# First context of a gated block: byte codes written in one operation into preset f16 words

## The reference, cut to what matters

```python
q1 = clip(round(layernorm(x) / s1 + z1), 0, 255)            # 2 x 1024 x 2048
q2 = clip(round(ctx / s2 + z2), 0, 255)                     # 2 x 2048 x 2048
x  = x + tanh(g_xattn) * ((q1 - z1) * s1) @ ((q2 - z2) * s2)
x  = x + tanh(g_ffn) * layernorm(x) @ ((U * S) @ V.T).T     # U, V: 2048 x 512
```

## Time and profile before

| | |
|---|---|
| median of 3 runs | 601.6 us (601.25 to 601.85) |
| span of the profiled execution | 600.8 us |
| TensorE busy | 583.0 us (97%) |
| VectorE, ScalarE, GpSimd busy | 384.5, 210.5, 193.5 us |
| first matmul | 11.34 us |

### The profile page before, as it was taken

How to read it: one execution, slowest core, us unless ns; L and a number is a source line. 1 busy time by engine, 2 the same in 40 slices (tenths; PEclk the granted TensorE clock), 3 DMA queues, 4 the chain that set the end, 5 groups by cost and what they waited for, 6 DMA issues and landing times.

```text
span 600.8 us, 7536 instructions
## 1 busy us (share of the span) xinstructions
PE 583.0 (97%) x2800; PEld 266.3 (44%) x2800; DVE 384.5 (64%) x703; ACT 210.5 (35%) x256; POOL 193.5 (32%) x149
## 2 busy tenths in 40 slices
PE   1999999999999999999999999999999999999998
PEld 0444444444444444445444444444444444444444
DVE  6968999995288962855266975647375665735212
ACT  4799877822041432476422220303011030301000
POOL 2998850002223419735505800210404030030000
PEclk9999999999999999999999999999999999999999
DMA  8999995539828896979934432360917355171512
GB/s 275 387 387 386 308 262 127 109 122 196 242 54 230 192 217 189 274 264 327 235 123 140 102 73 54 75 189 12 211 42 157 106 97 166 32 161 35 123 53 105
DMA packets 145940, 102.74 MB, mean 171 GB/s; under 512 B 108784, under 2 KB 109040, under 8 KB 145904
## 3 DMA queue, kind: packets, MB, share of 16 engines
q1 hardware_dynamic: 136912, 84.96, 53.6%
q10 hardware_dynamic: 8992, 17.30, 8.8%
HBM read 58.99 MB, written 16.78 MB: 126 GB/s over the span
## 4 chain that ended last, share of the span: by engine, by line
PE 74%; DVE 12%; DMA 7%; issue 3%; ACT 1%; SPq 1%; POOL 1%; ACTq 0%; DVEq 0%
PE bank L556 27%; PE bank L587 14%; PE bank L654 8%; PE bank L653 8%; PE bank L658 8%; PE bank L592 7%; DMA v_hl<-in_ctx_dram 4%; DVE u_hl L1249 2%; DVE ring L1134 2%; DVE xn L1171 1%; DVE xs L1174 1%; DVE v_hl L1243 1%; DMA qT<-qn 1%; PE bank L519 1%; DMA ring<-in_x_dram 1%
## 5 line engine op out<-in xcount | busy, mean ns | idle before, releaser
L556 PE MATMUL bank<-q,qT 128*128 128x512 bf16 x896 | 202.1, 381 | 0.6 <-DVE ring L1134 0.3
L556 PEld LDWEIGHTS bank<-q,qT 128*128 128x128 bf16 x896 | 87.7, 98 | 107.9 <-issue 1.8
L260 POOL TENSOR_SCALAR ring<-ring,bvec 128x2048 f32<-128x2048 f32 x16 | 33.3, 2084 | 270.2 <-DVE bvec L1116 270.2
L587 PE MATMUL bank<-v_hl,xT 128*128 128x512 f16 x512 | 115.8, 379 | 0.0
L265 POOL TENSOR_TENSOR ring<-ring,corr 128x512 f32<-128x512 f32 x64 | 88.7, 1417 | 24.6 <-ACT corr L851 23.6
L1134 DVE SCALAR_TENSOR_TENSOR ring<-bank,const,ring 128x512 f32<-128x512 f32 x64 | 47.6, 743 | 57.9 <-PE bank L556 57.8
L1207 DVE SCALAR_TENSOR_TENSOR ring<-bank,cy,ring 128x512 f32<-128x512 f32 x63 | 46.6, 747 | 56.7 <-PE bank L658 56.6
L654 PE MATMUL bank<-u_hl,hbuf 128*128 128x512 f16 x208 | 78.9, 380 | 0.0
L653 PE MATMUL bank<-u_hl,hbuf 128*128 128x512 f16 x208 | 78.9, 379 | 0.0
L254 POOL TENSOR_SCALAR q<-u8r,const 128x1024 bf16<-128x1024 uint8 x52 | 64.2, 1243 | 39.2 <-ACT u8r L757 35.6
L587 PEld LDWEIGHTS bank<-v_hl,xT 128*128 128x128 f16 x512 | 49.9, 98 | 59.9 <-DMA xT<-xs 0.5
(11 more groups left out here) (136 smaller groups left out, 524.9 us busy)
## 6 DMA issues: line engine op xcount, KB each, us to landing
out_dram<-ring SPq DMA_DIRECT2D x63, 256.0 KB, 3.6
ring<-in_x_dram SPq DMA_DIRECT2D x62, 256.0 KB, 4.1
v_hl<-in_ctx_dram SPq DMA_DIRECT2D x26, 512.0 KB, 11.5
stage<-in_ctx_dram ACTq DMA_DIRECT2D x17, 512.0 KB, 5.5
u_hl<-in_L_ffn_V_dram SPq DMA_DIRECT2D x8, 512.0 KB, 11.4
corr<-in_ctx_dram ACTq DMA_DIRECT2D x8, 512.0 KB, 6.1
stage<-in_ctx_dram SPq DMA_DIRECT2D x6, 512.0 KB, 11.4
q<-in_ctx_dram ACTq DMA_DIRECT2D x4, 512.0 KB, 10.1
```

Of the source, the lines that this page charges most:

```text
L556: mm = nc.tensor.matmul(unit_bank(t, n)[:, :], qT_of(t)[:, k, :], q2[:, n, k, :], start=(k == 0), stop=(k == KT - 1))
L587: nc.tensor.matmul(h_bank(u)[:, :], xT[:, g, half, k % 8, :], v_hl[:, k, 0, :], start=(g == 0 and a == 0 and half == 0), stop=False)
```

## The change

`q2` becomes f16. Ahead of its use every 16-bit word of `q2` is set to 0x6400, which is 1024 in f16. A whole number q from 0 to 255 in the low byte makes the word 1024 + q. So context 0 is converted by one operation, which writes the byte straight into every second byte of `q2` (`q2_low`), and the centre of context 0 and 1 is -1024 as the correction terms see it (`C_C2`).

- GpSimd presets `q2` by four memsets of 128 x 4096 f32 words (`fill(n)`, one for each column block): `fill(0)` and `fill(1)` right behind its small memsets, `fill(2)` and `fill(3)` behind chunk 5.
- One-operation conversions: ScalarE does chunks 6, 7, 8 and the even ones from 10 to 30 (`ON_ACT`, 14 of them), GpSimd chunks 0 to 5 and the odd ones from 9 to 31 (18).
- VectorE converts no chunk any more. It gets one more 128 x 1 operation in `ratios`.
- Context 1 goes as before through `u8r`, with `op2` now adding 1024 and writing f16.
- `qn`, `qT`, the identity and the ones are f16 too; the identity is no longer built a second time (L293 to L297 are gone). The parts of the column sums are scaled by 1/16 instead of 1/4.
- `load_chunk` waits for the one-operation conversion of chunk c - 10.

```diff
+    OFFSET = 1024.0
+    OFFSET_PAIR = 2.0 ** 73 * (1.0 + 200.0 / 2.0 ** 16)
...
-        q2 = sb("q2", [P, NQ, KT, W], bf16)
+        q2 = sb("q2", [P, NQ, KT, W], f16)
...
-        WHOLE = (27, 31)
-        POOL_WHOLE = (1, 2, 3, 4, 5)
+        ON_ACT = (6, 7, 8, 10, 12, 14, 16, 18, 20, 22, 24, 26, 28, 30)
...
+        q2_low = lambda c: q2_chunk(c).bitcast(u8).rearrange("p (w b) -> p w b", b=2)[:, :, 0]
...
+            def fill(n):
+                nc.gpsimd.memset(flat2(q2[:, n, :, :]).bitcast(f32), OFFSET_PAIR).then_inc(q2_filled, 1)
+
+            def op1(c):
+                pool.wait_ge(SPOT[c][1], LANDED[c])
+                pool.wait_ge(q2_filled, c // CQ + 1)
+                if c == 0:
+                    pool.wait_ge(centre_ready, 1)
+                nc.gpsimd.tensor_scalar(q2_low(c), flat2(SPOT[c][0]), C_R2, P_Z2, ALU.mult, ALU.add).then_inc(q2_pool, 1)
...
-            nc.gpsimd.memset(ones_h[:, :], 4.0 / GW).then_inc(setup_ready, 1)
-
+            nc.gpsimd.memset(ones_part[:, :], 16.0 / GW).then_inc(setup_ready, 1)
+
+            fill(0)
+            fill(1)
             for c in range(CQ):
-                if not on_dve(c):
-                    op2(c)
+                if c not in ON_ACT:
+                    op1(c)
+            fill(2)
+            fill(3)
             for n in range(NQ - 1):
-                for i, c in enumerate(range(CQ * (n + 1), CQ * (n + 2), 2)):
-                    op2(c)
+                for i, c in enumerate(range(CQ * (n + 1) + 1, CQ * (n + 2), 2)):
+                    op1(c)
...
@@ scalar
+                if c < CB:
+                    act.wait_ge(q2_filled, c // CQ + 1)
+                    nc.scalar.activation(q2_low(c), flat2(SPOT[c][0]), ACT.Identity,
+                                         bias=P_Z2, scale=C_R2).then_inc(q2_act, 1)
+                    return
...
             root1(0)
-            op1(0)
             act.wait_ge(centre_ready, 1)
             op2(0)
...
@@ vector
                 step(ts(C_C, C_C, MAGIC, None, ALU.subtract))
+                step(ts(C_C2, P_Z2, 0.0, -OFFSET, ALU.mult, ALU.add))
                 ts(C_NC, C_C, -1.0, None, ALU.mult).then_inc(centre_ready, 1)
...
             for n in range(NQ - 1):
-                for i, c in enumerate(range(CQ * (n + 1) + 1, CQ * (n + 2), 2)):
-                    op2(c)
-                    if n == 0 and i == 1:
-                        sums1(3)
-                        variance1(3)
-                    elif n == 0 and i == 3:
-                        quantise(3)
+                if n == 0:
+                    sums1(3)
+                    variance1(3)
+                    quantise(3)
```

More of the change, by code:

```diff
@@ L58, in gated_block_program @@
         corr = sb("corr", [P, D], f32)
-        qn = sb("qn", [P, D], bf16)
-        qT = sb("qT", [P, 2, KT, P], bf16)
+        qn = sb("qn", [P, D], f16)
+        qT = sb("qT", [P, 2, KT, P], f16)
         xn = sb("xn", [P, HW], f32)
@@ L66, in gated_block_program @@
         u8r = sb("u8r", [P, NU8, CK * W], u8)
-        ident_b = sb("ident_b", [P, P], bf16)
+        ident = sb("ident", [P, P], f16)
         ones_f = sb("ones_f", [P, P], f32)
-        ones_b = sb("ones_b", [P, P], bf16)
-        ones_h = sb("ones_h", [P, P], f16)
+        ones = sb("ones", [P, P], f16)
+        ones_part = sb("ones_part", [P, P], f16)
         par = sb("par", [P, 6 + RT], f32)
@@ L188, in gated_block_program @@
         part_count = lambda t, h=1: 2 * t + h + 1 if t < G else 2 * G + t - G + 1
-        WHOLE = (27, 31)
-        POOL_WHOLE = (1, 2, 3, 4, 5)
[L191 to L194, removed]
+        ON_ACT = (6, 7, 8, 10, 12, 14, 16, 18, 20, 22, 24, 26, 28, 30)
+        act_count = lambda c: sum(i <= c for i in ON_ACT)
+        pool_count = lambda c: c + 1 - act_count(c)
+        u8_count = lambda c: c - CB + 1
         unit_bank = lambda t, n: bank[4 * (n % 2) + t] if t < G else bank[(unit(t, n) - NQ * G) % 3]
@@ L291, in _ @@
                         op2(c)
[L292 to L297, removed]
                 if t not in (6, 7):
@@ L316, in load_chunk @@
                 b, n, i = chunk(c)
[L317 to L320, removed]
+                if c >= NST and c - NST in ON_ACT:
+                    sp.wait_ge(q2_act, act_count(c - NST))
                 elif c >= NST:
-                    sp.wait_ge(ctx_u8, act_u8(c - NST))
+                    sp.wait_ge(q2_pool, pool_count(c - NST))
                 sp.dma_start(SPOT[c][0], ctx_k[b, :, CK * i:CK * i + CK, n * W:(n + 1) * W]).then_inc(SPOT[c][1], 16)
@@ L518, in colsum @@
                     if b == 0:
-                        mm = nc.tensor.matmul(colsum_bank(b, n)[:, :], ones_b[:, :], q2[:, n, k, :],
+                        mm = nc.tensor.matmul(colsum_bank(b, n)[:, :], ones[:, :], q2[:, n, k, :],
                                               start=(k == 0), stop=(k == KT - 1))
@@ L522, in colsum @@
                         g = k % CG * GW
-                        mm = nc.tensor.matmul(colsum_bank(b, n)[g:g + GW, :], ones_b[:, g:g + GW], q2[:, n, k, :],
+                        mm = nc.tensor.matmul(colsum_bank(b, n)[g:g + GW, :], ones[:, g:g + GW], q2[:, n, k, :],
                                               start=(k < CG), stop=(k >= KT - CG), tile_position=(0, g))
@@ L531, in colsum_total @@
                 pe.wait_ge(parts_lo, n + 1)
-                nc.tensor.matmul(colsum_bank(1, n)[:, :], ones_h[:, :], part_hi(n), start=True, stop=False)
-                nc.tensor.matmul(colsum_bank(1, n)[:, :], ones_h[:, :], part_lo(n), start=False, stop=True)\
+                nc.tensor.matmul(colsum_bank(1, n)[:, :], ones_part[:, :], part_hi(n), start=True, stop=False)
+                nc.tensor.matmul(colsum_bank(1, n)[:, :], ones_part[:, :], part_lo(n), start=False, stop=True)\
                     .then_inc(colsum_summed, 1)
@@ L789, in qT_half @@
                 nc.scalar.activation(qT_of(t)[:, 8 * h:8 * h + 8, :].rearrange("p k w -> p (k w)"),
-                                     bank[4 + 2 * (t % 2) + h][:, :].bitcast(bf16), ACT.Copy).then_inc(t_read, 1)
+                                     bank[4 + 2 * (t % 2) + h][:, :].bitcast(f16), ACT.Copy).then_inc(t_read, 1)
             def root1(t):
@@ L910, in _ @@
             qT_half(2, 1)
-            for c in range(9, 14):
+            for c in (10, 12, 14):
                 op1(c)
             column_correction(0, 0)
-            op1(14)
             root1(3)
-            for c in range(15, 19):
+            for c in (16, 18):
                 op1(c)
             op2(3)
-            for c in range(19, 23):
+            for c in (20, 22):
                 op1(c)
             column_correction(0, 1)
-            for c in range(23, 27):
+            for c in (24, 26, 28, 30):
                 op1(c)
-            op1(28)
-            op1(29)
-            op1(30)
             column_correction(0, 2)
```

82 lines of the change are left out of this document (26 added, 56 removed).

## The result

The change costs **10.8 us**: 612.57 us (612.05 to 613.23, 4 runs) against 601.73 (601.25 to 602.82, 4 runs) in the same session, a ratio of 1.0178 [1.0164, 1.0192]. The forecast was 606.3, range 600.0 to 608.2. The direction was right, and the time lies 4.4 us above the range.

The account below looks back on a forecast made before the run. But for 0.6 us, the kernel was taken to be paid for in its first 23 us, before TensorE runs gapless. Terms: 5.3 - 0.6 = +4.7 us, span 605.5, plus 0.8 gives 606.3; range 600.0 to 608.2.

Parts of the forecast that it names:

- Fills: GpSimd's memsets of 4096 words: 3.5 us each, bounds 1.7 and 3.9; fill(0) ends at 5.4, fill(1) at 8.9.
- Fills hold VectorE: VectorE's tensor_scalar operations beside a fill: each waits the whole fill; bounds no wait or the whole fill.
- The rival that a memset holds nothing back: Start, L1052 at 5.6: fills do not delay VectorE, so the kernel gets 1.2 us faster, 600.4 us; chance 16%.
- the short fills: Rival on GpSimd's presets: fills take 1.7 us each, done by 5.4, giving 601.0 us; chance 6%.
- Start: VectorE behind fill(0) and fill(1): tile 0's statistics begin at 9.7, not 5.4; tile 1's quantise at 21.4.
- Conversions: GpSimd's one operation a chunk, writing every second byte: 1.19 us, bounds 1.11 and 2.3.
- Every second byte is dear: Rival on the chunk conversions: strided bytes take 2.3 us a chunk on both engines, 3 us on top, 609; chance 7%.
- The step that failed: VectorE's waiting tensor_scalar goes ahead of GpSimd's next operation; tile 1's second half, behind chunk 5, done at 23.9.
- a meeting that falls the other way: Tile 2's quantise waiting when fill(2) ends: one half 3 us sooner, half of that reaching the end; range's low end.
- The path to the end: Tile 2's late halves delay ScalarE's copies; TensorE stands at the ninth matmul until 37.4; chunk 7 at 38.7, +5.3 us.
- The small terms: TensorE's wait for VectorE's chunk goes, -0.6 us; no chunk waits between 40 and 75 us, none for GpSimd's chunks.
- Cost at nothing on GpSimd: Fills on GpSimd alone cost nothing, as it is idle there, waiting for chunk 0.

Follow-up runs that it names:

- best kernel: Changed kernel with single-column `ratios`, chunks 6 and 7 on GpSimd, fill(2) behind chunk 7 and tile 2's quantise, fill(3) behind chunk 17: 600.43 us, ratio 0.9977.
- twelfth run: Changed kernel with one wait added: GpSimd waits on its own semaphore for chunk 5 ahead of fill(2): 606.49 us, ratio to before 1.0076.
- kernel with both cures: Changed kernel with `ratios` in 128x1 operations and fill(2), fill(3) moved behind chunk 9 and tile 2's quantise: 602.07 us, ratio to before 1.0005.
- ninth kernel: The best kernel with fill(3) as VectorE's memset behind its last constants, instead of on GpSimd: 600.59 us, ratio 0.9976.

## Why the prediction was right and where it failed

- **Fills.** 3.5 us each, of a memset's slope: 6.98 and 6.95 for two. Right.
- **Fills hold VectorE.** The decisive term of the sign, taken from no direct row: right for `tensor_scalar` on two or more columns. The rival that a memset holds nothing back falls with L1039's 3.44 us, and the short fills fall too. The Trainium skill ("SBUF — State Buffer", Who interferes with whom) says that the one that issues first has the shared ports for its whole instruction and the other fully blocks; the rows agree inside a memset, which lasts 3.49 us. By the rows' starts they do not agree at the seam behind chunk 5: the half stood from 22.13, fill(2)'s row begins at 23.22, and the fill went first.
- **Start.** Statistics of tile 0 at 9.7 foreseen, at 9.51 measured; quantise of tile 1 at 21.4 and 21.27.
- **Conversions.** 1.19 us for a strided byte: 1.20 measured, 1.20 without the stride. "Every second byte is dear" falls.
- **The step that failed** is the rule that the waiting operation "waits until GpSimd's operation is over, and then goes ahead of GpSimd's next", applied to tile 1's second half: done at 23.9, it said; 30.7 it was. The rule had been read from GpSimd's conversions, and between two of these it holds (1.62 us for the half in the best kernel). Behind a conversion with a fill next it does not hold (8.59 us). That seam alone is worth 6.1 us (the twelfth run), all of what the forecast was short. I had named a meeting that falls the other way, but only for tile 2 and only as a gain, so the range had no room for it above.
- **The path to the end.** The forecast let it run over tile 2's copies, with TensorE standing at the ninth matmul. The chain of waits of after runs over tile 1 (start, duration, what):

```profile
21.27 9.46 DVE qn L1092 x2
...
30.75 1.25 ACT qn L771 x2
...
32.05 1.03 PE bank L489 x8
33.08 2.61 PE bank L549 x6
```

  From 32.05 on TensorE has no gap: all that had queued up behind tile 1's half takes it to chunk 7 at 44.72, 12.7 us, and tile 2, though ScalarE begins its second copy only at 42.20 and not at 36.4, is in time. 1.7 of the 12.7 are the clock: 1.27 on six matmuls and 0.41 on eight transposes (1.03 us, where those of tile 1's first half took 0.62). The forecast had the clock only as a possibility above its sum. So 6.8 us on VectorE became 6.0 at chunk 7.
- **The small terms.** VectorE's chunk wait of 0.6 us is gone, and no chunk is waited for after 40 us: right. That TensorE would wait "no longer for GpSimd's chunks" was wrong by the forecast's own path, which had chunk 0 done at 10.9: the wait ahead of the first matmul is still 11.0. No half of tile 2 lasted 2.5 to 3 us, since the fills were over by then; in the twelfth kernel the first lasts 3.22. The stand at tile 2's ninth matmul did not come, for the reason just given.
- **Span and time.** The span was foreseen at 605.5 and is 610.7, 5.2 more; the time was missed by 6.3. The forecast added 0.8 us for what lies around a span. In every profile with a known time it is 1.8 (612.51 against 610.7, 606.73 against 604.9), so the profiled execution of before took about 602.6 by this estimate, 1.0 above the median, and the spans show the miss too small by that. From median to median 4.7 us were foreseen and 10.8 came: 6.1 more.
- **Cost at nothing on GpSimd.** Nothing in after speaks against it: GpSimd was idle at the start, and in the middle the tiles were later still. Once these are in time, the kernel with both cures is 1.2 us above the one without presets, with waits for GpSimd's `pre` in it.

In the times of the runs: no meetings 600.9; the start's alone 604.5, the middle's alone 605.1; both, with a turn for VectorE between chunk 5 and fill(2), 606.5; without that turn 612.6.

## What to carry to other kernels

A GpSimd operation that reads nothing and lies in its idle time is not free: list VectorE's `tensor_scalar` operations beside it with two or more elements a partition, and who waits for them. Put long fills where VectorE's work has slack, cut VectorE's few-element operations to one column, or put a wait for GpSimd's own last operation ahead of a fill, which cost GpSimd 0.4 us (fills of 7.38 instead of 6.95) and gave 6.1 us here. A rule on who goes first should be read from a row with the same two kinds of operation on both sides of the seam, and where there is none, the range takes the whole train behind it, to the far side too.

## What the hardware showed that I had not expected

- The seam rule: a half was kept out of two memsets in a row, and out of sixteen of 512 words (8.72 us for 0.8 us of work), when its wait began in a conversion; a gap ended that, which in the rows of the twelfth kernel is 0.06 us (chunk 5 ends at 23.13, fill(2) begins at 23.19).
- A `tensor_scalar` on one column does not wait for a memset at all (0.14 to 0.15 us), one on two columns does (up to 4.45 us). It is not the columns alone: the reciprocal of the scales, on two columns, runs in 0.17 us at 4.17, in the midst of fill(0). `BATCH_NORM_STATS2` ran at 2.47 us for four beside a fill, as without.
- VectorE writes 128 x 4096 words in 3.47 us, GpSimd in 3.49 to 3.51. I had expected 4.3 to 4.5 on VectorE.
- A wait for a semaphore that has been reached already makes no gap: in the ninth kernel one stood between chunk 7 and fill(2), for a half that ended 1.0 us before the fill began (25.27 and 26.28), and L1059 was kept out for the whole fill.
